# Self and causal attention of a 12-stage decoder: head rows stacked through a DRAM image, heads on the row halves

## The chip, the cores and the metric

The kernel runs on one core of a Trainium2 chip. The metric is the device time of one execution, in microseconds (us); it is a median of several runs. A core has five engines that work side by side, each through its own list of instructions in order, and wait for one another on semaphores: TensorE (PE; matmuls into PSUM, which has eight banks of 2 KB per partition), VectorE (DVE), ScalarE (ACT), GpSimd (POOL) and SyncE (SP, which here only starts DMA transfers). PEld is TensorE's loading of the stationary operand, which runs beside its matmuls.

## The reference

A decoder of four layers on x of 4 batches x 512 positions x 128 features. Each layer has three steps (an attention, a step with the context, a feed-forward part), and each step ends with `x = layernorm(x + step(x))`. Two of the twelve steps concern us, both with 16 heads of width 8: the attention of layer 1 (plain) and that of layer 3 (causal, with a softmax of its own).

```python
q, k, v = heads(x @ w_q), heads(x @ w_k), heads(x @ w_v)      # (4, 16, 512, 8)
attn = einsum('bhqd,bhkd->bhqk', q, k) * 8 ** -0.5
# layer 1: softmax(attn)
# layer 3: attn = where(causal, attn, -inf); a = clip(attn, -100, 100); m = max(a)
#          e = exp(a - m); p = e / (sum(e) + 1e-6) + 1e-8; p = p / sum(p)
out = merge_heads(einsum('bhqk,bhkd->bhqd', p, v)) @ w_proj
```

## The kernel before

The twelve steps are stages, one after the other. `attention16` is the stage of both attentions: "l1a" in the names of its tiles is the self attention (about 284 to 589 us of the profile), "l3a" the causal one (about 1486 to 1804). Constants for both are made in the first stage, the charge attention ("l0a").

**Numbers in three parts.** The scores are made by bf16 matmuls, although q and k are f32. So q and k of a batch are split into three bf16 parts, high, middle and low (tile `parts`), and a head's score is the sum of six products of parts. These lie under each other in the contraction: a head takes 64 rows, eight of width 8, six with products, one for the row maximum, one empty. Two heads, a pair, fill the 128 rows of QS (queries) and KS (keys). In KS each head of a pair has a copy of its own in which the other head's 64 rows are zero; a matmul over 128 rows then gives one head's scores.

**Units.** A batch has 4 groups of 4 heads (2 pairs); with 4 batches a stage has 16 groups, m = 0 to 15. The work is cut into units, and each engine goes through the same list of units:
- J: projections of a batch. J0 and J1 make q and k (f32 matmuls), J2 makes v, and along them ScalarE and VectorE make the three parts; J4 makes the last low part; J3 (causal) sums v.
- Q and K (L586): the rows of one pair are put in their places. Three matmuls with a constant 0/1 matrix (`k.gather`) move the parts to their rows in PSUM; ScalarE copies them to QS (L742) and KS (L753, L755), in the self attention VectorE copies the second half of KS (L843).
- A (L611): scores of 128 queries against all keys, for the two heads of a pair, into two banks; VectorE takes the row maxima (L855). The causal one has fewer keys and adds a mask (L613).
- P, T: the four heads' maxima are split into three parts (L867 to L873), turned by TensorE (L619) and added into the row of QS meant for them (L878, "the T addition").
- B (L640): scores of one head, transposed, 128 keys against all queries, with the maximum subtracted in the matmul; ScalarE takes the exponential (L773). The units alternate over banks 4 and 5, and a B waits until the exponential of the B two earlier is made. L (causal) makes a lower bound in the same way, X clips (L883).
- V (L671): the exponentials times v, four heads on four column quarters of the array. F, C, W, Y, N: transposes, output projection, norm.

**The order.** `FULL` and `CAUSAL` list the units of a group by hand: kind, how many groups ahead, which. A unit `('A', 2, 0, 1)` in group m is an A of group m + 2. `FULL_BATCH` and `CAUSAL_BATCH` put the units of a batch between them: key m % 4, position, unit. So J of the next batch stands in groups with m % 4 == 2, Q and K are made two groups ahead. Banks 0/1 and 2/3 alternate between A and T units: an A waits until VectorE has read the A or T two earlier.

SP, which issues most transfers, has nothing to do in these two stages.

Of the kernel before, what the change touches and what calls it, by code (L numbers as in the profile page):

```python
# [13 lines left out]
ALU = mybir.AluOpType  # L14
ACT = mybir.ActivationFunctionType
# [18 lines left out]
BIAS_ROWS = (0, 64, 96)  # L34
SCALE = DK ** -0.5
# [144 lines left out]
class Dispatch:  # L180
# [163 lines left out]
)  # L344
CAUSAL_BATCH = {
    1: ((17, ('C', -1)),),
    2: ((1, ('J', 1, 0)), (8, ('J', 1, 1)), (10, ('J', 1, 2)), (16, ('J', 1, 3)), (17, ('J', 1, 4)), (38, ('W', -1)),),
    3: ((6, ('Y', -1)), (17, ('N', -1)),),
# [8 lines left out]
)  # L357
FULL_BATCH = {
    1: ((30, ('C', -1)),),
    2: ((0, ('J', 1, 0)), (2, ('J', 1, 1)), (3, ('J', 1, 2)), (4, ('J', 1, 4)), (32, ('W', -1)),),  # L360
    3: ((23, ('Y', -1)), (32, ('N', -1)),),
# [3 lines left out]
def attention16(k, name, w, cross=None, mask=None, causal=False):  # L365

    nc, PS = k.nc, k.PS
    crossed = cross is not None
    KT = [(0, SC)] if crossed else [(t * P, P) for t in range(NT)]  # L380
    nk = KT[-1][0] + KT[-1][1]
    LIM = 100.0 / SCALE
    ROUND = len(KT)
    NG = BT * G
    AHEAD = 3 if crossed else 2

    def a_units(m):
        if m >= NG:
            return []
        return [("A", m, 0, hp) for hp in range(2)] if crossed else [("A", m, qt, hp) for qt in range(NT) for hp in range(2)]  # L390

    def gathers(m):
        if m >= NG:
            return []
        if crossed:
            return [("Q", m, 0)] + ([("K", m, 0)] if m % 2 == 0 else [])
        return [(c, m, i) for i in range(2) for c in "QK"]

    def projections(b):
        return [("J", b, i) for i in range(4 if causal else 3)] if b < BT else []  # L400

    def extras(m):
        b, g = m // G, m % G
        put = gathers(m + AHEAD)
        old = b - 1 if b else None
        u = [("F", m - 2)] if m >= 2 else []
        if g == 0:
            u += put + projections(b + 1)
        if g == 1:
            u = ([("J", b + 1, 4)] if b + 1 < BT else []) + u + put + ([("C", old)] if b else [])  # L410
        if g == 2:
            u += put + ([("W", old)] if b else [])
        if g == 3:
            u += ([("Y", old)] if b else []) + put + ([("N", old)] if b else [])
        return u

    def spread(base, more):
        o, put = [], 0
        for i, u in enumerate(base):
            while put < len(more) and i * (len(more) + 1) >= (put + 1) * len(base):  # L420
                o.append(more[put])
                put += 1
            o.append(u)
        return o + more[put:]

    order = projections(0) + [("J", 0, 4)]
    early = [u for m in range(AHEAD) for u in gathers(m)]
    if crossed:
        order += early + a_units(0) + [("P", 0)] + a_units(1) + [("T", 0)]
    else:  # L430
        order += early[:4]
        rest = early[4:]
        for u in a_units(0):
            order += [u] + rest[:1]
            rest = rest[1:]
        order += rest + [("P", 0), ("T", 0)]
    head = len(order)
    for m in range(NG if crossed else 0):
        base = []
        nxt = a_units(m + 2)  # L440
        base += [("P", m + 1)] if m + 1 < NG else []
        base += [("B", m, 0, 0)] + nxt[:1] + [("B", m, 0, 1)]
        base += [("T", m + 1)] if m + 1 < NG else []
        base += [("V", m - 1, 0, 1)] if m else []
        base += [("B", m, 0, 2)] + nxt[1:] + [("B", m, 0, 3)]
        order += spread(base, extras(m))
    if crossed:
        order += [("F", NG - 2), ("V", NG - 1, 0, 1), ("F", NG - 1)]
    else:
        group, batch = (CAUSAL, CAUSAL_BATCH) if causal else (FULL, FULL_BATCH)  # L450
        done = set(order)
        for m in range(-1, NG + 2):
            for i, (kind, ahead, *which) in enumerate(group):
                for at, (what, later, *part) in batch.get(m % G, ()) if 0 <= m < NG else ():
                    if at == i and 0 <= m // G + later < BT:
                        order.append((what, m // G + later, *part))
                u = (kind, m + ahead, *which)
                if 0 <= m + ahead < NG and u not in done:
                    order.append(u)
    order += [(c, BT - 1) for c in "CWYN"]  # L460
    count = lambda kinds: {u: i for i, u in enumerate([u for u in order if u[0] in kinds])}
    in_pairs = "ATQ" if crossed else "AT"
    ua, ut = count(in_pairs), count("AT")
    first_a, last_a = {}, {}
    for u in ut:
        if u[0] == "A":
            first_a.setdefault(u[1], u)
            last_a[u[1]] = u
    ub, uq, uk, uj = count("BL"), count("QK"), count("K"), count("J")
    pairs = [u for u in order if u[0] in in_pairs]  # L470
    singles = [u for u in order if u[0] in "JQKFCWN" and u not in ua and u[0:1] + u[2:] != ("J", 4)]
# [5 lines left out]
    last_b = lambda m: ub["B", m, len(KT) - 1, HG - 1]  # L477
    gathered = {b: max(i for u, i in uq.items() if u[1] // G <= b) + 1 for b in range(BT)}
    sets = 2 if crossed else 3
    freed = {}  # L480
# [5 lines left out]
    def body(block, projected, high_made, rest_made, middle_made, low_made, zeroed, v_taken, stack_ready, taken_a,  # L486
# [22 lines left out]
        def keys(m):  # L509
            return KS[:, m // G % 2 if crossed else 0]  # L510

        @block.tensor
        def _(pe):
# [3 lines left out]
            def emptied(u):  # L517
# [5 lines left out]
                if kind == "J" and u[2] == 2:  # L523
                    pe.wait_ge(v_taken, m + 1)
# [3267 lines left out]
```

## Time and profile before

| | |
|---|---|
| time, median of 3 runs | 2075.52 us (2074.79 to 2079.33) |
| profiled execution, span from first to last instruction | 2076.9 us |
| TensorE busy | 1713.3 us, 82% |
| VectorE busy | 1420.7 us, 68% |
| ScalarE busy | 1103.9 us, 53% |
| GpSimd busy | 412.8 us, 20% |
| mean granted TensorE clock | 0.912 of full speed |

The profile is of one execution. Its own time is the span; nothing else of it is shown around the span, and it lies 1.4 us over the median. Busy time is the union of an engine's instructions; matmuls are pipelined, so TensorE counts as busy while the tail of a matmul runs beside the next one. The granted clock has two levels, 0.5 (1.2 GHz) and 1.0 (2.4 GHz); values between are means. The shares are means over twelve stages with different limits, so the stages concerned have to be read by themselves.

### The profile page before, as it was taken

How to read it: one execution, taken by the hardware profiler on the slowest of the kernel's cores; microseconds unless marked ns; L12 is line 12 of the kernel's file. 1: busy time of each engine (PE TensorE's matmuls, PEld its weight loads, DVE VectorE, ACT ScalarE, POOL GpSimd, SP SyncE). 2: the span in 40 equal slices, each digit the busy share in tenths (PEclk: the TensorE clock that was granted, in tenths of full speed). 3: DMA queues.
4: the chain of work that ended last, by engine and by line, in shares of the span. 5: the costliest groups of instructions: out<-in, count | busy, mean ns of one | idle time of the engine just before them, and what ended most of it. 6: DMA issues, size and time to landing. Idle time of an engine off the chain costs nothing. (4 is left out here: it accounts for less than half of the span.)

```text
span 2076.9 us, 33295 instructions
## 1 busy us (share of the span) xinstructions
PE 1713.3 (82%) x11716; PEld 1018.4 (49%) x11806; DVE 1420.7 (68%) x3271; ACT 1103.9 (53%) x2329; POOL 412.8 (20%) x576
## 2 busy tenths in 40 slices
PE   5779869999968999994879899984489889798692
PEld 3546533333356666662734445442344445465572
DVE  4646677888765777774746767676789999666434
ACT  3436536777723444544445555652368778375362
POOL 0110030000032666653100000001300000100375
PEclk8989879999978999996979999997699999899696
DMA  4000000000025888861000000000000000000313
GB/s 123 1 1 2 1 1 1 1 1 1 1 92 217 311 327 325 331 253 42 1 0 1 1 1 1 1 1 18 0 1 2 1 1 2 1 2 7 101 52 85
DMA packets 38398, 120.09 MB, mean 58 GB/s; under 512 B 6610, under 2 KB 22139, under 8 KB 33147
## 3 DMA queue, kind: packets, MB, share of 16 engines
q1 hardware_dynamic: 28059, 104.78, 14.0%
q0 software_dynamic: 4992, 10.23, 1.6%
q10 hardware_dynamic: 5184, 2.95, 0.5%
q8 instruction: 97, 1.59, 0.3%
q14 instruction: 66, 0.54, 0.1%
HBM read 108.08 MB, written 14.58 MB: 59 GB/s over the span
## 5 line engine op out<-in xcount | busy, mean ns | idle before, releaser
L160 POOL TENSOR_SCALAR rstd<-MV 128x2 f32<-128x2 f32 (+1 forms) x100 | 25.7, 257 | 1014.9 <-DVE MV L128 1010.1
L855 DVE TENSOR_REDUCE l1aM<-PS 128x2 f32<-128x1024 f32 x128 | 152.9, 1220 | 24.1 <-PE PS L611 22.1
L773 ACT ACTIVATE l1aE<-PS 128x512 f32<-128x512 f32 x256 | 140.8, 595 | 48.3 <-PE PS L640 45.0
L773 ACT ACTIVATE l3aE<-PS 128x512 f32<-128x512 f32 (+3 forms) x256 | 102.5, 443 | 46.9 <-PE PS L644 43.9
L2737 ACT COPY PT<-PS 128x512 f32<-128x512 f32 x128 | 69.2, 589 | 93.6 <-PE PS L2648 93.3
L855 DVE TENSOR_REDUCE l3aM<-PS 128x2 f32<-128x256 f32 (+3 forms) x128 | 101.1, 818 | 18.8 <-PE PS L613 17.7
L2827 DVE TENSOR_REDUCE M<-PS 128x1 f32<-128x589 f32 x128 | 92.4, 763 | 27.1 <-PE PS L2637 26.8
L1868 PE MATMUL PS<-WB,H 128*128 128x512 f32 x234 | 109.0, 602 | 0.0
L2743 ACT ACTIVATE E<-PS,M 128x589 f32<-128x589 f32 x128 | 95.8, 762 | 17.6 <-DVE M L2827 17.5
L883 DVE SCALAR_TENSOR_TENSOR l3aE<-l3aE,l3aLB 128x2048 f32<-128x2048 f32 (+1 forms) x64 | 94.9, 1483 | 2.7 <-ACT l3aE L773 2.7
L2008 ACT ACTIVATE H<-PS,WB 128x128 f32<-128x128 f32 x156 | 44.5, 368 | 89.3 <-PE PS L1856 89.2
L611 PE MATMUL PS<-l1aKS,l1aQS 128*128 128x512 bf16 x249 | 77.4, 391 | 16.1 <-DVE l1aQS L878 5.5
L640 PE MATMUL PS<-l1aQS,l1aKS 128*128 128x512 bf16 x239 | 82.3, 387 | 5.4 <-ACT l1aE L773 4.2
L2665 PE MATMUL PS<-PT,Va 128*64 128x512 f32 x320 | 82.8, 616 | 0.8 <-ACT Q L2748 0.8
L2648 PEld LDWEIGHTS PS<-cols_const_sb,E 128*128 128x128 f32 x512 | 58.2, 144 | 49.6 <-DVE E L2847 29.4
L162 POOL TENSOR_TENSOR rstd<-rstd,mhalf 128x2 f32<-128x2 f32 (+1 forms) x100 | 75.8, 758 | 8.3
L2637 PE MATMUL PS<-K,Q 64*128 64x512 f32 x256 | 75.1, 664 | 0.0
L2021 ACT ACTIVATE A<-PS,WB 128x128 f32<-128x128 f32 x156 | 58.7, 457 | 29.3 <-PE PS L1878 29.3
L2648 PE MATMUL PS<-cols_const_sb,E 128*128 128x128 f32 x512 | 71.4, 283 | 2.8 <-DVE E L2847 2.6
L640 PE MATMUL PS<-l3aQS,l3aKS 128*128 128x512 bf16 (+3 forms) x254 | 70.3, 305 | 3.3 <-ACT l3aE L773 1.7
L2847 DVE TENSOR_SCALAR E<-E,sums 128x589 f32<-128x589 f32 x128 | 67.6, 528 | 4.5
L611 PE MATMUL PS<-l3aKS,l3aQS 128*128 128x256 bf16 (+3 forms) x248 | 62.3, 304 | 8.9 <-DVE l3aM L855 5.6
(687 smaller groups left out, 4502.8 us busy)
## 6 DMA issues: line engine op xcount, KB each, us to landing
WB<-in_experts SPq DMA_DIRECT2D x39, 1286.0 KB
TB<-mixed_tails SPq DMA_DIRECT2D x39, 768.5 KB, 7.1
ALL<-in_experts SPq DMA_DIRECT2D x8, 384.0 KB, 6.5
mixed_tails<-in_tails SPq DMA_DIRECT2D x1, 2305.5 KB, 11.9
cols_fold_sb<-in_cols_fold SPq DMA_DIRECT2D x1, 1676.0 KB, 11.5
mixed_tails<-in_tails SPq DMA_DIRECT2D x1, 1537.0 KB, 16.1
mixed_tails<-WB SPq DMA_DIRECT2D x2, 768.5 KB, 4.6
cols_l2x_sb<-in_cols_l2x SPq DMA_DIRECT2D x1, 1154.0 KB, 10.9
```

The costliest lines, as they stand in the source:

```text
L162: g.tensor_tensor(out, out, self.mhalf[:, 0:out.shape[1]], ALU.pow).then_inc(done, 1)
L611: ins = mm(o, QS[:, pp, qt * P:(qt + 1) * P], keys(m)[:, pp, par, 0:kc], start=True, stop=not causal)
L640: ins = mm(o, keys(m)[:, pp, par, k0:k0 + kn], QS[:, pp, q0:S], start=True, stop=not (mask or causal))
L773: nc.scalar.activation(E[0:kn, home(m, kt) + j, q0:S], PS[0:kn, 4 + n % 2, q0:S], ACT.Exp, scale=SCALE).then_inc(exp_done, 1)
L855: v.tensor_reduce(M[:, m % 2, qt, 2 * hp:2 * hp + 2], PS[:, bank:bank + 2, 0:kc], AX, ALU.max, negate=True).then_inc(pair_free, 1)
L883: v.scalar_tensor_tensor(e, e, 1.0, LB[:, m % 2, :, kt * P:S], ALU.min, ALU.max).then_inc(clipped, 1)
L1868: mm(o, H1[:, i % 3, c * P:(c + 1) * P], mid_w(i, c), start=False, stop=False)
L2637: ins = mm(PS[:, at_ + 2 * par, :], Q[own, b % 2, pp, q], K[own, b % 2, pp, :], start=True, stop=True)
L2648: ins = nc.tensor.transpose(PS[:, at_ + 2 * par, t * P:(t + 1) * P], E[:, ring(x, par), e0:e0 + P], k.ident)
L2665: ins = mm(PS[64 * par:64 * par + 64, 6, :], Va[:, b % 2, t, h * DH:(h + 1) * DH], PT[:, n % 2, par, t, :], start=(t == 0), stop=(t == len ...
L2743: nc.scalar.activation(E[:, i, 0:NK], scores(s, par), ACT.Exp, bias=M[:, i:i + 1], accum_out=sums[:, i:i + 1]).then_inc(exp_done, 1)
L2827: ins = v.tensor_reduce(M[:, i:i + 1], scores(s, par), AX, ALU.max, negate=True)
```

## The change

Q and K units go, with the constant matrices. The parts are written by SP to an image in DRAM, `k.image[batch, q or k, head, d, slot, position]` in bf16, each part to the slots that need it (`IMAGE_SLOTS`: the high part of q to slots 0, 3 and 6, and so on; one transfer writes a part to all its slots). Rows of 1 KB. Then SP reads a group's rows back, already stacked: one transfer of 256 KB into QS, one of 256 KB (self) or two of 128 KB (causal) into KS. The slots 5 and 7 are filled once, in the first stage: zeros for q and for k's slot 7, in k's slot 5 ones for d < 3 and zeros otherwise. An A waits on its group's transfers. The reads of group m + 4 wait until the B of group m are done.

In the self attention KS loses its zero halves: A and B of a head work on 64 of the 128 rows, the first head of a pair on rows 0 to 63, the second on 64 to 127. The causal one keeps the 128 rows.

J moves from groups with m % 4 == 2 to those with m % 4 == 1; the v projection is now J5, behind most of the group's units. The other units keep their order.

```diff
+IMAGE_SLOTS = (((0, 3, 6), (1, 4), (2,)), ((0, 1, 2), (3, 4), (6,)))
+AUG_SLOT = 5
 CAUSAL_BATCH = {
-    1: ((17, ('C', -1)),),
-    2: ((1, ('J', 1, 0)), (8, ('J', 1, 1)), (10, ('J', 1, 2)), (16, ('J', 1, 3)), (17, ('J', 1, 4)), (38, ('W', -1)),),
+    1: ((11, ('J', 1, 0)), (13, ('J', 1, 1)), (15, ('J', 1, 2)), (17, ('J', 1, 4)), (17, ('C', -1)), (20, ('J', 1, 5)), (24, ('J', 1, 3))),
+    2: ((34, ('W', -1)),),
 FULL_BATCH = {
-    1: ((30, ('C', -1)),),
-    2: ((0, ('J', 1, 0)), (2, ('J', 1, 1)), (3, ('J', 1, 2)), (4, ('J', 1, 4)), (32, ('W', -1)),),
+    1: ((0, ('J', 1, 0)), (2, ('J', 1, 1)), (3, ('J', 1, 2)), (4, ('J', 1, 4)), (24, ('J', 1, 5)), (26, ('C', -1))),
+    2: ((28, ('W', -1)),),
...
+    rows_of = lambda par: slice(0, P) if causal else slice(64 * par, 64 * par + 64)
+    order = [("J", 0, i) for i in (0, 1, 2, 4, 5)] + [("J", 0, 3)] * causal
+    order += [("A", 0, qt, hp) for qt in range(NT) for hp in range(2)] + [("P", 0), ("T", 0)]
...
+        KS = k.sb(name + "KS", [P, H // 2, 2, S] if causal else [P, H // 2, S], BF16)
+        @block.sync
+        def _(sp):
+            sp.wait_ge(k.blanked, 16 * 2 * BT)
+            for m in range(NG):
+                b, g = divmod(m, G)
+                if g == 0:
+                    for part, made in enumerate((high_made, middle_made, low_made)):
+                        for c in range(2):
+                            slots = IMAGE_SLOTS[c][part]
+                            step = slots[1] - slots[0] if len(slots) > 1 else 1
+                            rows = k.image[b, c, :, :, slots[0]:slots[-1] + 1:step, :].rearrange("h d j s -> (h d) j s")
+                            sp.wait_ge(made, 2 * b + c + 1)
+                            sp.dma_start(rows, parts[:, c, part:part + 1, :].broadcast_to([P, len(slots), S])).then_inc(imaged[c], 16)
+                    sp.wait_ge(q_imaged, PARTS * (b + 1))
+                    sp.wait_ge(k_imaged, PARTS * (b + 1))
+                if m >= G:
+                    sp.wait_ge(s_ready, last_b(m - G) + 1)
...
+                sp.dma_start(QS[:, own, :], k.image[b, 0, heads].rearrange("(a r) d j s -> (r d j) a s", r=2)).then_inc(stacked[g], 16)
+                if causal:
+                    for par in range(2):
+                        sp.dma_start(KS[64 * par:64 * par + 64, own, par, :], key[par]).then_inc(stacked[g], 16)
+                else:
+                    sp.dma_start(KS[:, own, :], k.image[b, 1, heads].rearrange("(a r) d j s -> (r d j) a s", r=2)).then_inc(stacked[g], 16)
...
                 elif kind == "A":
+                    pe.wait_ge(stacked[g], ROWS * (m // G + 1))
-                            ins = mm(o, QS[:, pp, qt * P:(qt + 1) * P], keys(m)[:, pp, par, 0:kc], start=True, stop=not causal)
+                        own = rows_of(par)
+                        key = KS[:, pp, par, :] if causal else KS[own, pp, :]
+                        ins = mm(o, QS[own, pp, qt * P:(qt + 1) * P], key[:, 0:kc], start=True, stop=not causal)
...
+        def blank_image(sp):
+            sp.wait_ge(blank_made, 1)
+            for b in range(BT):
+                for c in range(2):
+                    sp.dma_start(k.image[b, c, :, :, AUG_SLOT:DK:2, :].rearrange("h d j s -> (h d) j s"), blank[:, c]).then_inc(k.blanked, 16)
...
-            terms = one.enter_context(nc.sbuf_tensor("terms", [P, 6 * P + 2 * P + H // 2 + 1], F32))
+            terms = one.enter_context(nc.sbuf_tensor("terms", [P, 2 * P + 1], F32))
+            blank = one.enter_context(nc.sbuf_tensor("blank", [P, 2, 2, S], BF16))
```

B changes as A does. In the first stage ScalarE's eight multiplications that made the gather matrices (L3550) go, VectorE makes one small addition for the fill, GpSimd zeroes it at the start, and the load `terms` shrinks from 516.5 KB to a quarter. In l1a GpSimd no longer zeroes KS.

## Rows read from the trace of the kernel before

**Rows 1.** Busy time: us; PE, PEld, DVE, ACT, POOL (count); granted clock, DMA, GB/s

```profile
313.00:575.00 262.00, 239.95 (x1404) 96.94 (x1430) 216.78 (x307) 187.64 (x345) 5.60 (x12) 0.98 0.00 1
...
1519.00:1790.00 271.00, 245.26 (x2326) 132.08 (x2362) 249.85 (x419) 203.65 (x432) 5.86 (x12) 0.99 0.01 1
```

**Rows 2.** T addition (L878): ns min/median/max, first and last start

```profile
L878 DVE TENSOR_TENSOR l1aQS<-PS,l1aQS x16: 1212/1214/1225, 309.8 to 560.7; 128x1024 bf16<-128x1024 f32 x16
```

**Rows 3.** Busy time of l1a, from one T addition to the next

```profile
395.61:411.19 15.58, 14.50 (x86) 5.51 (x86) 13.45 (x18) 11.29 (x22) 0.00 (x0) 1.00 0.00 1
411.19:431.12 19.93, 18.02 (x104) 7.91 (x106) 16.64 (x23) 14.36 (x27) 0.00 (x0) 1.00 0.00 1
431.12:448.23 17.11, 15.96 (x100) 7.07 (x101) 16.42 (x33) 12.05 (x23) 1.86 (x4) 1.00 0.01 2
```

**Rows 4.** Timeline of TensorE, plain l1a group: start, us, engine, line, out<-in, xcount

```profile
397.85 1.92 PE L671 MATMUL PS<-l1aE,l1aVa 128*32 128x512 f32 x16
...
399.93 0.59 PE L611 MATMUL PS<-l1aKS,l1aQS 128*128 128x512 bf16 x2
400.36 0.38 PE L640 MATMUL PS<-l1aQS,l1aKS 128*128 128x512 bf16 x1
400.58 0.81 PE L586 MATMUL PS<-l1aparts,gather 128*128 128x512 bf16 x3
```

**Rows 5.** Timeline of VectorE in l1a; in brackets idle before and releaser

```profile
317.17 1.23 DVE L855 TENSOR_REDUCE l1aM<-PS 128x2 f32<-128x1024 f32 x1 [2.69 <-PE PS L611]
...
400.56 1.22 DVE L855 TENSOR_REDUCE l1aM<-PS 128x2 f32<-128x1024 f32 x1 [1.48 <-PE PS L611]
...
404.62 0.76 DVE L843 TENSOR_SCALAR l1aKS<-PS,isaug 64x512 bf16<-64x512 f32 x1
405.41 2.36 DVE L855 TENSOR_REDUCE l1aM<-PS 128x2 f32<-128x1024 f32 x2
...
420.37 0.68 DVE L812 TENSOR_TENSOR l1aparts<-l1aleft,l1aparts 128x512 bf16<-128x512 f32 x1
```

**Rows 6.** Busy time of a plain group of l3a

```profile
1653.47:1669.40 15.93, 14.75 (x147) 7.84 (x148) 14.94 (x25) 12.71 (x27) 0.00 (x0) 1.00 0.01 1
```

**Rows 7.** Timeline of VectorE in that l3a group

```profile
1657.69 0.42 DVE L855 TENSOR_REDUCE l3aM<-PS 128x2 f32<-128x256 f32 x1 [0.64 <-PE PS L613]
```

**Rows 8.** Timeline of TensorE in the latent attention

```profile
1201.06 1.13 PE L2601 MATMUL PS<-LT,cols_l2x_sb 128*128 128x512 f32 x2
...
1205.44 0.23 PE L2634 MATMUL PS<-kmask_b,ones_b 128*128 128x154 bf16 x1
1205.61 0.70 PE L2637 MATMUL PS<-K,Q 64*128 64x512 f32 x2
```

**Rows 9.** Timeline of the head of l1a

```profile
291.91 0.68 DVE L812 TENSOR_TENSOR l1aparts<-l1aleft,l1aparts 128x512 bf16<-128x512 f32 x1
...
295.78 0.59 PE L611 MATMUL PS<-l1aKS,l1aQS 128*128 128x512 bf16 x2 [0.94 <-DVE l1aKS L843]
...
313.01 1.06 PE L640 MATMUL PS<-l1aQS,l1aKS 128*128 128x512 bf16 x2
```

**Rows 10.** DMA issues: queue, count, KB each, us to landing

```profile
expert_rows<-X SPq DMA_DIRECT2D x1, 1024.0 KB, 6.4
...
terms<-in_terms ACTq DMA_DIRECT2D x1, 516.5 KB
...
cols_l3a_sb<-in_cols_l3a SPq DMA_DIRECT2D x1, 257.0 KB, 2.9
```

**Rows 11.** Timeline, end of the charge attention and start of the next stage

```profile
134.19 1.76 ACT L3550 ACTIVATE gather<-terms 128x768 bf16<-128x768 f32 x2
...
136.24 1.37 PE L989 MATMUL PS<-CT,cols_l0x_sb 128*128 128x308 f32 x2 [2.57 <-PEq L87]
```

**Rows 12.** Waits at the start: who for whom, us, times, longest

```profile
PE PS L3500 <- DMA X<-in_x: 10.5, 1, 10.5
```

**Rows 13.** Busy time of a stretch of the charge attention

```profile
60.00:80.00 20.00, 14.74 (x93) 10.76 (x92) 12.71 (x34) 8.57 (x15) 2.18 (x4) 1.00 0.01 1
```

More of the change, by code:

```diff
@@ L399, in projections @@
[L399 to L436, printed above, removed]
@@ L437, in attention16 @@
-    head = len(order)
[L438 to L459, printed above, removed]
@@ L460, in attention16 @@
-    order += [(c, BT - 1) for c in "CWYN"]
[L461 to L471, printed above, removed]
+    PARTS = 3 * 16
@@ new lines, in attention16 @@
+    ROWS = 3 * 16 if causal else 2 * 16
+    rows_of = lambda par: slice(0, P) if causal else slice(64 * par, 64 * par + 64)
+    order = [("J", 0, i) for i in (0, 1, 2, 4, 5)] + [("J", 0, 3)] * causal
+    order += [("A", 0, qt, hp) for qt in range(NT) for hp in range(2)] + [("P", 0), ("T", 0)]
+    head = len(order)
+    group, batch = (CAUSAL, CAUSAL_BATCH) if causal else (FULL, FULL_BATCH)
+    done = set(order)
+    for m in range(-1, NG + 2):
+        for i, (kind, ahead, *which) in enumerate(group):
+            for at, (what, later, *part) in batch.get(m % G, ()) if 0 <= m < NG else ():
+                if at == i and 0 <= m // G + later < BT:
+                    order.append((what, m // G + later, *part))
+            u = (kind, m + ahead, *which)
+            if 0 <= m + ahead < NG and u not in done:
+                order.append(u)
@@ L472, in attention16 @@
+    order += [(c, BT - 1) for c in "CWYN"]
+    count = lambda units: {u: i for i, u in enumerate(units)}
+    ut, ub = (count([u for u in order if u[0] in kinds]) for kinds in ("AT", "BL"))
+    uj = count([u for u in order if u[0] == "J" and u[2] not in (2, 4)])
+    pairs = list(ut)
+    last_a = {u[1]: u for u in ut if u[0] == "A"}
+    singles = [u for u in order if u in uj or u[0] in "FCWN"]
     ring = (7, 4, 5, 6)
@@ L526, in emptied @@
                     pe.wait_ge(v_summed, m + 1)
-                if kind in "QK":
-                    pe.wait_ge(taken_a, uq[u] + 1)
-                if kind == "K" and not causal:
-                    pe.wait_ge(taken_v, uk[u] + 1)
                 if kind in "AT":
@@ L572, in _ @@
                         ins.then_inc(projected, 1)
-                elif kind in "QK":
-                    b, isk = m // G, int(kind == "K")
-                    for part, made in enumerate((high_made, middle_made, low_made)):
-                        pe.wait_ge(made, 2 * b + isk + 1)
-                    if not crossed:
-                        outs = [(2 * g + u[2], PS[:, own, 0:width[isk]])]
-                    elif isk:
-                        outs = [(2 * g + i, PS[:, own, i * nk:(i + 1) * nk]) for i in range(HG)]
-                    else:
-                        outs = [(2 * g + i, PS[:, bank + i, :]) for i in range(2)]
-                    for pp, o in outs:
-                        for part in range(3):
-                            ins = mm(o, k.gather[:, pp, isk, part, :], parts[:, isk, part, 0:width[isk]],
-                                     start=(part == 0), stop=(part == 2))
-                    ins.then_inc(stack_ready, 1)
@@ L589, in _ @@
                 elif kind == "A":
                     _, _, qt, hp = u
-                    if ut[u] == 0:
-                        pe.wait_ge(zeroed, 2)
-                    if u == first_a[m]:
-                        mine = [x for x in gathers(m) + (gathers(m - 1) if crossed and m % 2 else [])]
-                        pe.wait_ge(taken_a, max(uq[x] for x in mine) + 1)
-                        if not causal:
-                            pe.wait_ge(taken_v, max(uk[x] for x in mine if x in uk) + 1)
@@ new lines, in _ @@
+                    pe.wait_ge(stacked[g], ROWS * (m // G + 1))
+                    pp = 2 * g + hp
+                    kc = (qt + 1) * P if causal else S
+                    for par in range(2):
+                        o = PS[:, bank + par, 0:kc]
+                        own = rows_of(par)
+                        key = KS[:, pp, par, :] if causal else KS[own, pp, :]
+                        ins = mm(o, QS[own, pp, qt * P:(qt + 1) * P], key[:, 0:kc], start=True, stop=not causal)
+                        if causal:
+                            ins = mm(o[:, qt * P:kc], k.ident_b, k.causal_b, start=False, stop=True)
@@ L757, in _ @@
+                        nc.scalar.copy(parts[:, i - 1, 1, :], left[:, i - 1, :]).then_inc(middle_made, 1)
                 elif kind in "BL":
@@ L865, in _ @@
                     maxima, rest = (a.rearrange("p t (a r) -> p a t r", a=2) for a in (Mg, Mleft[:, :, :]))
-                    high, middle, low = (Mp[:, :, :, 32 + i:P:64] for i in range(3))
+                    high, middle, low = (Mp[:, :, :, DK * i + AUG_SLOT:P:64] for i in range(3))
                     step(v.tensor_copy(high, maxima))
```

266 lines of the change are left out of this document (83 added, 183 removed), and 14 rows, old and new, of tables (CAUSAL, FULL).

## The prediction

> **What bounds the kernel now.** The changed function runs twice: the self attention (stage l1a) and the causal attention (l3a). First I read the sums by stretch [rows 1]: over its steady part l1a has TensorE busy 240 of 262 us and VectorE 217; l3a has VectorE busy 250 of 271 and TensorE 245. A busy TensorE overstates itself, because matmuls overlap. So next comes the period. Each of the 16 groups has one T addition on VectorE, the first at 309.8 and the last at 560.7 us [rows 2], 250.9 us for 15 intervals. Cut at these additions there are three kinds [rows 3]: a plain group takes 15.6 us (nine of them, 15.1 to 15.6), one with the next batch's projections 19.9 (three, and the first group of the stage takes 19.8), the one after that 17.1 (two); the last takes 13.1.
>
> For a plain group of l1a the starts on TensorE give what each unit holds the engine for [rows 4]: an A pair 0.43 us (399.93 to 400.36), a B 0.22 (400.36 to 400.58), a gather three times that, 0.65, a V of 16 matmuls 1.9. With 8 A, 16 B, 4 gathers and 2 V that is 3.4 + 3.5 + 2.6 + 3.8 = 13.3 us, before the short transposes of T and F: TensorE is nearly full. VectorE in the same group is busy 13.45 us [rows 3] and waits in two places for A's matmuls; the long wait, 1.48 us at 400.56, is the time that the V ahead of that A takes [rows 5]. So a plain l1a group is held by TensorE, with VectorE two microseconds behind. In l3a a plain group of 15.93 us has VectorE busy 14.94 [rows 6], with one visible wait of 0.64 [rows 7]: there VectorE is the bound.
>
> **What the change takes away.** Per group and stage: 12 gather matmuls (2.6 us of TensorE), two ScalarE copies to QS, and in l1a two ScalarE and two VectorE copies to KS; in l3a four ScalarE copies. VectorE's copies take 0.76 us each; the one at 404.62 holds VectorE to 405.41, so 0.79, 1.55 to 1.6 per group [rows 5]. In l3a VectorE loses nothing.
>
> In l1a a pair of A, and neighbouring B of a pair, use the array's two row halves. Does that run side by side? The latent attention already has it, in f32: two 64-row matmuls of 512 columns take 0.70 us together, two full-array ones of as many columns 1.13 [rows 8]. So the second starts about 0.1 us after the first and not after its whole pass. For the bf16 A pair I take 0.1 to 0.2 us off 0.43.
>
> Here a rule speaks against the change. In the rows the switch from a 128-row to a 64-row matmul costs nothing visible: the 128-row one starts at 1205.44 and lasts 0.23, the 64-row pair starts at 1205.61 [rows 8]. The Trainium skill (TensorEngine Tiling (Array Packing), Tiling Modes, Key Properties) says that a change of tiling mode drains the engine. By it T and F, neighbours in the order, would be one more stretch in another mode, two more changes per l1a group; the time that this would give stands with the rivals.
>
> **The sum for l1a.** A plain group: minus 1.55 (K copies). The 1.48 wait stays for the most part, since the V in front of that A is unchanged and only the A pair and the B pair before it and the A pair itself get shorter: three times 0.1 to 0.2, I take 0.5. Together minus 2.1, nine times: minus 19. Bounds: minus 1.0 (a third of the copies' time comes back as new waits) and minus 3.3 (the copies, and nearly all 2.1 us of idle [rows 3]). The three groups with projections: VectorE is busy 16.64 of 19.93 and its gaps are the to and fro with ScalarE over the three-part split, which stays; minus 1.8 each, 5.4. The two after them: VectorE busy 16.42 of 17.11, so only the copies go: minus 1.6 each, 3.2. The first group waits longer (2.69 us at 317.17 [rows 5]): minus 2.5. The last: minus 0.3. Sum minus 30.
>
> **The head of a stage** gets longer. Before, the last low part is made at 292.6 (291.91 + 0.68) and the first A starts at 295.78 [rows 9]. After, six image writes of 1536 KB in all go out behind the parts, then two reads of 256 KB. Nearest rows: a write of 1024 KB lands in 6.4 us, a read of 257 KB in 2.9 [rows 10]. 768 KB (the high parts) leave before the middle parts are made, so I let the writes end 4 us after the last low part (between 2.5 and 8, the latter at 1024 KB per 6.4 us with no head start), and the reads 4 us later (the second queues behind the first): first A at 300.6, 5 us late. From there the head is shorter: the first B came 17.2 us after the first A [rows 9], with four gathers and two K copies (1.6 us of VectorE) among the A units, which go. Net plus 3 (0 to plus 8). In l3a, where VectorE had nothing to lose but waited for the gathers, plus 0.5 (minus 1 to plus 4), kept inside that stage's term.
>
> At the later batches the round trip is hidden. The projections move one group forward. Before, the last low part came about 10 us after the T that opens the interval (420.37 plus 0.68 against 411.19 [rows 3, 5]; the VectorE copy of V ahead of it is moved behind): then 8 us for write and read give 18 us. The first A of the next batch is due just before the end of the interval after, 18 + 13 - 3 = 28 us after that T. Cover: some 10 us; if the round trip grows by more, VectorE stands still there. The reads of the other groups are issued when the B of the group four earlier are done, more than one period before they are needed. SP has nothing else in these stages; behind its waits stand only its own image transfers. Three transfers a group on l3a, two on l1a, cost the computing engines nothing but a wait on a semaphore.
>
> **l3a.** VectorE is full, so only its waits can go: 0.64 in a plain group [rows 7]. ScalarE loses its copies (off the path), TensorE 2.6 us; the A units come earlier. I take a half, with the longer waits of the three batch groups: minus 4 (plus 4 to minus 10).
>
> **Edges.** Eight ScalarE multiplications that made the gather matrices go. The last two stand between the charge attention's last copy and its end: 1.76 us from 134.19, and the next stage's first matmul at 136.24 had waited for that [rows 11]: minus 1.7. The others lie beside TensorE work. Added there are one small VectorE addition (hidden, the engine then waits for ScalarE), a GpSimd fill at the start, idle otherwise, and eight fills of the image, 2 MB, with the DMA engines idle and hundreds of microseconds of cover. At the start the first matmul waits 10.5 us for x [rows 12] while a load of 516.5 KB shares the DMA engines; 388 KB of it go, 2.4 us at the rate of the 1024 KB write [rows 10] and nothing if the two don't meet: I take minus 0.7, nearer to nothing, because it is one of many loads.
>
> **Together**: -30 + 3 - 4 - 2.4 = -33 us on the profiled execution, whose span is 2076.9 us with nothing to add around it that the profile shows; it lies 1.4 us over the median of the runs, 2075.5. Forecast: 2042 us.
>
> **Rivals.**
> (1) *VectorE closes up.* TensorE, some 10 us of work in a 13 us group, runs ahead, and the wait behind V goes too: 3.3 in nine groups, 3 in the three with projections, l3a minus 8: about 2020. For it: TensorE gets 4 us of slack. Against: units stand in a written order, and A behind V can't be moved forward. 0.22.
> (2) *Waits come back.* B alternates over two banks and each waits for the exponential two earlier; A stands behind B in the order, so the freed VectorE time turns into waits for A: minus 1 a group, nothing in l3a, heads 3 us longer each: 10 + 4 + 6 more, 2062. 0.16.
> (3) *Slower: the round trip is late.* The place is the first A of each batch. It decides from 18 us for write and read (8 estimated, 10 of cover). At 26 us six batches stand still for 8 us, and the two heads 18 us longer: 48 + 36 more, 2126; at 18 the heads alone take 20 of the 33, and from about 20 us the kernel is slower than before. For it: 128 KB and 256 KB transfers in rows of 1 KB, a write and a read that must follow each other. Against: the 1024 KB write of 6.4 us has rows of 512 bytes. 0.05.
> (4) *Slower: the clock falls.* At 1.2 GHz TensorE would need twice its 9.8 us and the transposes twice, 21 us where 15.6 sufficed: over l1a plus 88 in place of minus 30, 2160. It decides from somewhat over a quarter of the stage. Against: with TensorE busy 14.7 of 20 us, 74%, the granted clock was 1.00 [rows 13], about the share that I expect (10 of 13.4). 0.04.
> (5) *The halves don't overlap, or the mode change costs.* Without overlap (the change then does not do what it says) the 0.5 per group and as much in the others is lost: 2048. A drain, priced by the tail of a matmul (0.38 long, the next after 0.22 [rows 4]: 0.16), is 0.3 us a group with two more changes, 5 us in 16: 2047 if TensorE is on the path there. Both together 0.10. This second part is what the named rule of the Trainium skill would give.
>
> The forecast itself has 0.43. Its own range is 2031 to 2051; over all, 2018 to 2064 leaves out (3), (4) and the outer parts of (1) and (2). A difference of under 0.2%, 4 us, is what a measurement can't tell from none. Faster by more: (1), (5), the forecast and nearly all of (2): 0.88. Slower: (3), (4) and a little of (2): 0.09. Same: 0.03.
>
> **What would show it.** Right: T additions of l1a 13.3 to 13.7 us apart in plain groups, with one VectorE wait of about a microsecond behind V; the two matmuls of an A starting about 0.1 us apart; l3a plain groups still 15.4 to 15.9; the first A of l1a some 8 us after the last low part (3.2 before), and no later wait of A for a DMA; granted clock 1.00 between. Wrong: plain groups over 14.5, TensorE waiting for the stacked rows at the batch changes, or a granted clock well under 0.9.

## The result and the profile after

The changed kernel takes 2061.5 us (median of four runs, 2060.1 to 2070.3) where the kernel before takes 2077.4 beside it: ratio 0.9928, 95% interval 0.9909 to 0.9947. It is faster by 0.7%, about 16 us; forecast were 33, to 2042. The profiled execution of the changed kernel has a span of 2068.3 us; it is the longest of the four, so the stages below are compared by their own landmarks and not by the span.

The landmarks are the T additions again, now L733. In both kernels there are sixteen in each stage, and fifteen intervals between them: in the self attention (l1a) these sum to 224.6 us after 250.9, in the causal attention (l3a) to 273.2 after 262.6. So one stage gained 26.3 us and the other lost 10.6: together 15.7, about the difference of the medians. Each sum is of one execution.

These are the busy times of the changed kernel between T additions (us; PE, PEld, DVE, ACT, POOL with counts; granted clock, DMA share, GB/s): in l1a a plain group, the group with the projections and the one behind it, which answer to [rows 3]; then in l3a a plain group, which answers to [rows 6], a group with the projections, and a second plain group.

```profile
372.58:385.25 12.67, 10.99 (x78) 3.65 (x76) 11.61 (x17) 9.25 (x18) 0.00 (x0) 1.00 0.13 41
385.25:404.01 18.76, 13.89 (x78) 4.02 (x76) 14.35 (x21) 11.26 (x21) 0.00 (x0) 0.91 0.35 114
404.01:419.14 15.13, 13.15 (x92) 5.09 (x92) 12.39 (x17) 10.06 (x19) 0.00 (x0) 1.00 0.12 36
1563.94:1580.07 16.13, 13.47 (x139) 7.35 (x137) 14.94 (x24) 9.49 (x23) 0.00 (x0) 0.96 0.11 34
1580.07:1606.93 26.86, 19.54 (x160) 11.18 (x160) 19.80 (x33) 11.74 (x26) 0.00 (x0) 0.87 0.24 79
...
1641.48:1656.97 15.49, 12.70 (x136) 6.86 (x136) 14.74 (x25) 9.04 (x22) 0.00 (x0) 1.00 0.13 35
```

A plain l1a group fell from 15.58 to 12.67 us; of the five plain groups left in the stage four take 12.7 to 12.8, the fifth, at a granted clock of 0.88, 14.32. The first plain l3a group shown did not fall: VectorE is busy 14.94 us in it, exactly as in [rows 6], and the clock is 0.96. The second took 15.49 us, 0.44 less than before, at a clock of 1.00. Most of them had a clock of 0.90 to 0.96 and took 15.9 to 16.5 us. The causal projection group takes 26.86 us; before, the three of that stage took 21.7 to 21.9. Its excess over a plain group nearly doubled, and the granted clock in it is 0.87 (over the stage's intervals 0.92, before 0.98).

TensorE and VectorE in the plain l1a group (timeline: start, us, engine, line, out<-in, xcount, in brackets idle before and releaser), which answer to [rows 4] and [rows 5]:

```profile
374.39 1.92 PE L578 MATMUL PS<-l1aE,l1aVa 128*32 128x512 f32 x16
376.25 0.39 PE L551 MATMUL PS<-l1aQS,l1aKS 64*128 64x512 bf16 x1
...
380.58 0.39 PE L521 MATMUL PS<-l1aKS,l1aQS 64*128 64x512 bf16 x2
380.81 0.38 PE L551 MATMUL PS<-l1aQS,l1aKS 64*128 64x512 bf16 x1
```

```profile
376.90 2.50 DVE L710 TENSOR_REDUCE l1aM<-PS 128x2 f32<-128x1024 f32 x2 [0.83 <-PE PS L521]
```

The two matmuls of an A pair, one on each row half, take 0.39 us together, as long as one alone; on the full array a pair took 0.59 [rows 4]. VectorE's wait behind V fell from 1.48 to 0.83 us.

At the heads the first A waits for the stacked rows. This is who TensorE waits for (us in total, times, longest), the two rows with the image:

```profile
PE PS L521 <- DMA l1aKS<-head_image: 9.1, 1, 9.1
PE PS L521 <- DMA l3aKS<-head_image: 4.1, 1, 4.1
```

It happens once in each stage; at the later batches TensorE never waits for the image. The wait for x at the start fell from 10.5 [rows 12] to 9.7, and at the end of the charge attention the multiplications of [rows 11] are gone: ScalarE's last copy starts at 135.80, takes 0.58, and the next stage's first matmul follows at 136.69, 0.31 us after the copy's end (before 1.96).

### The profile page after: what moved, and what is told of

Same layout as the page of the kernel before. It is cut to its first block and busy times, and to the rows that moved or that the text cites. A ratio compares the mean times of both kernels' runs of the same rounds, so it can differ in the third digit from the quotient of the medians.

```text
span 2068.3 us, 32399 instructions
## 1 busy us (share of the span) xinstructions
PE 1655.5 (80%) x11422; PEld 981.1 (47%) x11422; DVE 1393.1 (67%) x3239; ACT 1006.6 (49%) x2161; POOL 407.1 (20%) x573
## 5 line engine op out<-in xcount | busy, mean ns | idle before, releaser
L710 DVE TENSOR_REDUCE l3aM<-PS 128x2 f32<-128x256 f32 (+3 forms) x128 | 100.1, 817 | 14.6 <-PE PS L523 14.6
L2597 ACT ACTIVATE E<-PS,M 128x589 f32<-128x589 f32 x128 | 95.8, 762 | 17.6 <-DVE M L2681 17.5
L551 PE MATMUL PS<-l1aQS,l1aKS 64*128 64x512 bf16 x256 | 83.9, 405 | 20.2 <-ACT l1aE L649 17.4
L551 PE MATMUL PS<-l3aQS,l3aKS 128*128 128x512 bf16 (+3 forms) x256 | 76.0, 319 | 10.8 <-ACT l3aE L649 10.1
L521 PE MATMUL PS<-l1aKS,l1aQS 64*128 64x512 bf16 x256 | 61.5, 426 | 23.3 <-DVE l1aM L710 9.5
L521 PE MATMUL PS<-l3aKS,l3aQS 128*128 128x128 bf16 (+3 forms) x256 | 66.5, 315 | 14.8 <-DVE l3aM L710 9.5
```

Source lines behind the costliest of these rows:

```text
L521: ins = mm(o, QS[own, pp, qt * P:(qt + 1) * P], key[:, 0:kc], start=True, stop=not causal)
L551: ins = mm(o, key[:, kt * P:(kt + 1) * P], QS[own, pp, q0:S], start=True, stop=not causal)
L710: v.tensor_reduce(M[:, m % 2, qt, 2 * hp:2 * hp + 2], PS[:, bank:bank + 2, 0:kc], AX, ALU.max, negate=True).then_inc(pair_free, 1)
L2597: nc.scalar.activation(E[:, i, 0:NK], scores(s, par), ACT.Exp, bias=M[:, i:i + 1], accum_out=sums[:, i:i + 1]).then_inc(exp_done, 1)
```

## Where the causal stage lost it

TensorE and VectorE in the causal projection group of the changed kernel, the waits and what stands around them:

```profile
1587.70 1.13 PE L500 MATMUL PS<-XT,cols_l3a_sb 128*128 128x512 f32 x2 [1.97 <-DVE R L759]
...
1590.48 1.10 PE L500 MATMUL PS<-XT,cols_l3a_sb 128*128 128x512 f32 x2 [0.95 <-DVE l3aleft L683]
...
1600.50 2.05 PE L508 MATMUL PS<-l3aVa,cols_const_sb 128*128 128x128 f32 x8 [2.93 <-DVE l3aVa L694]
...
1603.77 1.93 PE L578 MATMUL PS<-l3aE,l3aVa 128*32 128x512 f32 x8
```

```profile
1596.47 2.28 DVE L738 SCALAR_TENSOR_TENSOR l3aE<-l3aE,l3aLB 128x2048 f32<-128x2048 f32 x1
...
1599.67 0.68 DVE L694 COPY l3aVa<-PS 128x512 f32<-128x512 f32 x1
...
1606.93 1.22 DVE L733 TENSOR_TENSOR l3aQS<-PS,l3aQS 128x1024 bf16<-128x1024 f32 x1 [2.39 <-PE PS L529]
```

Two places of the hand-written list show. First, q's projection (place 11) stands right behind F (place 10). Both use PSUM bank 7, so TensorE stands 1.97 us until VectorE has read F's result (its last reading instruction writes R, L759), and k's projection then 0.95 us for q. Second, the sum of v (L508, place 24) needs VectorE's copy of v (L694). That copy has its place behind the clip X (2.28 us) and the split of the maxima, so TensorE stands 2.93 us; every B behind it waits too, and at the end VectorE itself waits 2.39 us for the T matmuls.

The granted clock falls inside that second wait, which begins at 1597.57 and ends at 1600.50 (busy times as above):

```profile
1596.00:1598.00 2.00, 1.56 (x18) 0.73 (x16) 2.00 (x2) 1.37 (x4) 0.00 (x0) 1.00 0.38 124
1598.00:1601.00 3.00, 0.50 (x2) 0.53 (x3) 2.83 (x8) 0.38 (x1) 0.00 (x0) 0.74 0.28 78
1601.00:1604.00 3.00, 2.85 (x18) 2.02 (x20) 2.19 (x4) 0.82 (x3) 0.00 (x0) 0.50 0.30 99
```

So the wait has a second price: the eight matmuls of V behind it take 1.93 us, where in a projection group of the kernel before, at a clock of 1.00, they took 1.06.

A projection group and the one behind it take 40.5, 43.3 and 41.3 us at the three batch changes, where before a plain group and the projection group behind it took 37.0, 37.7 and 37.7: 12.8 us more. The other nine intervals of the stage gave 2.1 back.

The theory: these places are the loss. Rivals: (a) TensorE, thinner by the gathers, is granted a lower clock there, and that alone is the loss; (b) the image's transfers in that group delay something.

## The experiments

All are edits of the changed kernel. The table has, for each, the sum of the fifteen intervals of each stage in its profiled execution, the median and the ratio to the kernel before on the same chip.

| kernel | l1a sum | l3a sum | median, us | ratio (95% interval) |
|---|---|---|---|---|
| before | 250.9 | 262.6 | 2077.4 | 1 |
| changed | 224.6 | 273.2 | 2061.5 | 0.9928 (0.9909 to 0.9947) |
| a: projections ahead of F | 224.6 | 264.1 | 2056.3 | 0.9887 (0.9852 to 0.9921) |
| b: only q, k ahead of F | 224.3 | 269.4 | 2057.7 | 0.9892 (0.9864 to 0.9920) |
| c: only v a group later | 224.7 | 264.7 | 2050.1 | 0.9877 (0.9841 to 0.9912) |
| d: causal A twice | 224.7 | 278.3 | 2067.0 | 0.9948 (0.9930 to 0.9966) |
| f: b and c together | 224.5 | 261.7 | 2053.3 (1 run) | |
| g: zero halves, l1a | 223.0 | 273.0 | 2056.9 | 0.9929 (0.9901 to 0.9957) |
| h: image written twice | 220.9 | 270.9 | 2067.2 (1 run) | |
| i: late subtraction, v later | 214.4 | 267.5 | 2050.5 | 0.9896 (0.9869 to 0.9923) |
| l: l1a A twice | 218.5 | 272.9 | 2054.3 | 0.9889 (0.9860 to 0.9918) |
| j: i's l1a, f's l3a | 214.7 | 261.9 | 2041.5 | 0.9834 (0.9808 to 0.9860) |
| k: j, l1a A twice | 218.7 | 264.3 | 2043.3 | 0.9834 (0.9805 to 0.9863) |

Medians of one kernel's runs scatter by 5 us and more, so most intervals overlap; the sums of a stage whose code is untouched repeat within a microsecond in all kernels but h (3.7 and 2.3 off) and k (2.4 off in l3a), and they carry the verdicts. A difference of 2 to 4 us between two sums, such as b's, is therefore near to what one execution can be off. In the diffs a unit is written short, J0 for `('J', 1, 0)`.

**a, all projections ahead of F.**

```
-    1: ((11, J0), (13, J1), (15, J2), (17, J4), (17, C), (20, J5), (24, J3)),
+    1: ((1, J0), (3, J1), (5, J2), (6, J4), (6, J5), (9, J3), (17, C)),
```

> Causal attention only: in the group of the projections all six steps of the next batch's projections are put ahead of F (places 1 to 9 of the group's list in place of 11 to 24), among them v and its sum. Theory (the place costs: q and k wait for F's reading of PSUM bank 7, the sum of v waits 2.93 us for VectorE's copy of v behind the clip and the maxima's split): the three projection groups of the causal stage, 24.21, 26.86 and 25.77 us in the changed kernel, fall to about 21.8 each, as before; the stage's sum of intervals 273.2 -> about 262, the kernel 2061.5 -> about 2050. Rival one (TensorE, thinner without the gathers, is granted .87 of its clock there, and this alone makes the groups long): the groups stay at 24 to 27 and the clock at about .87; about 2061. Rival two (the transfers of the image in that group delay something): they are as many and start earlier, 2060 to 2062.

The three groups took 21.42, 23.67 and 23.66 us, the stage 264.1: 9.1 of the 10.6 us are back, with the place alone. The clock in the middle one rose from 0.87 to 1.00 without any work added. Together with the fall inside the wait, shown above, that says that there it followed the waits:

```profile
1574.87:1598.54 23.67, 17.31 (x160) 9.82 (x160) 19.64 (x34) 12.45 (x28) 0.00 (x0) 1.00 0.27 90
```

**b and c, the two places apart.** b has J0, J1, J2, J4 as in a, and J5, J3 at 20 and 24; c has the first four as in the changed kernel and J5, J3 in the next group:

```
+    2: ((1, J5), (6, J3), (34, W)),
```

> Causal attention only: of the projections' steps, q and k with their splits are put ahead of F (places 1 to 6), v and its sum stay at places 20 and 24. Theory: TensorE's waits at q and k (1.97 and 0.95 us in one group) go, the wait of 2.93 us for the copy of v stays; each projection group shorter by 2 to 3 us, 2061.5 -> about 2054. If the place of v is the whole cause: 2060 to 2062. If the clock is the cause: 2060 to 2062.

> Causal attention only: q and k stay where the change put them (places 11 to 17 of the group), v and its sum move to the next group, places 1 and 6, ahead of that group's F. Theory: the wait of 2.93 us for the copy of v goes with the slow 1.93 us of the products of V behind it, the projection group falls by about 4.5 us, the next one, which now has v's copy and two additions, grows by about 2.5; three times -2, 2061.5 -> about 2055. If q and k's waits behind F are the whole cause: the sum of the two groups stays, 2060 to 2062. If the clock is the cause: 2060 to 2063.

b gives 3.8 us of the stage and c 8.5. In c the projection group falls from 26.86 to 21.65 and the next grows from 16.39 to 18.06. TensorE's waits in the causal stage, first of the changed kernel, then of c, show which went:

```profile
PE PS L508 <- DVE l3aVa L694: 9.9, 3, 4.1
...
PE PS L500 <- DVE R L759: 3.9, 2, 2.0
...
PE PS L500 <- DVE l3aleft L683: 2.8, 3, 0.9
```

```profile
PE PS L500 <- DVE R L759: 3.9, 2, 2.0
...
PE PS L500 <- DVE l3aleft L683: 2.8, 3, 0.9
```

The 9.9 us for the copy of v are gone in c, the others stand as they were. So the place of v is the larger part, about two thirds, and the wait behind F the smaller. Both include what the clock gives back: in c's three projection groups it is 0.94 to 1.00, in the changed kernel 0.86 to 0.93.

**f, both.** J0, J1, J2, J4 at places 1, 3, 5, 6; J5, J3 in the next group at 1 and 6.

> Causal attention only: q and k ahead of F in the projection group (places 1 to 6) and v with its sum in the next group, ahead of its F (places 1 and 6). If the waits for F and for v are separate terms, the projection group falls to about 20 to 21 and the next one holds 18; the sum of the stage's intervals 262 or a little less (273.2 in the changed kernel, 264.1 and 264.7 with one remedy each); the kernel about 2050. If one remedy already took what the other would take: 264 to 265, about 2052.

261.7: the two remedies, 3.8 and 8.5, give 11.5 together, nearly their sum. They are separate terms. The stage is then as long as before (262.6) and no shorter.

**d, the clock by itself in the causal stage.**

```
-        ins = mm(o, QS[own, pp, ...], key[:, 0:kc], start=True, stop=not causal)
+        for again in range(2 if causal and g in (1, 2) else 1):
...
+            ins = mm(o, QS[own, pp, ...], key[:, 0:kc], start=True, stop=not causal or not last)
```

> Causal attention only: in the groups that issue their A products for heads groups 1 and 2 each product of a pair is computed twice into the same bank (the first result is written over), which keeps TensorE busy where the gathers did before. Rival one (the granted clock is the cause): the clock in the projection groups rises from .87 towards .97, and they fall by 2 us or more each; 2061.5 -> about 2055. Theory (place): the clock may rise, but the waits for F and for v stay, the groups stay within 1 us or grow with the products' own time; 2061 to 2068.

The middle group took 28.08 us, at a clock of still 0.87; the stage's mean rose from 0.92 to 0.94 and its sum by 5.1 us. In the first projection group the clock did rise, from 0.86 to 0.93, and the group stayed as long (24.13 us after 24.21). As a test of the clock this is inconclusive: in the middle group it didn't move, and the added products take time themselves.

**g, self attention with zero halves.** KS has two images again, each product runs over 128 rows; stacking and order stay.

```
-    rows_of = lambda par: slice(0, P) if causal else slice(64 * par, 64 * par + 64)
+    rows_of = lambda par: slice(0, P)
...
```

> Self attention only: the keys keep two images with a zero half each and every product runs over all 128 rows, as in the causal attention; the stacking through DRAM and the order stay. Theory (two products on the row halves run side by side, 0.39 us for both): eight pairs a group cost 0.43 to 0.59 us more each on TensorE, which is busy 10.99 of 12.67 us, so a plain group grows to about 14 to 14.5, the stage by about 20 us, and the kernel goes from 2061.5 to about 2080. Rival (VectorE sets the plain group at 12.7 and TensorE has room): plain groups 12.7 to 13, the kernel 2061 to 2066.

Both theories failed. A plain group took 13.53 us, 0.86 more, but the projection groups took 17.1 to 17.6 in place of 18.8 to 19.7, and the sum is 223.0 against 224.6. The row halves give nothing in the sum here, although the pair is faster on them. The projection group of g and the plain one before it:

```profile
368.85:382.38 13.53, 12.57 (x76) 4.37 (x77) 11.74 (x17) 9.38 (x18) 0.00 (x0) 1.00 0.13 39
382.38:399.94 17.56, 14.38 (x78) 4.76 (x77) 14.34 (x20) 11.55 (x21) 0.00 (x0) 1.00 0.37 121
```

VectorE has the same work (14.34 us against 14.35); the clock is 1.00 where the row halves had 0.91. In the changed kernel one V of that group takes 3.14 us, in g each takes 1.92.

**l, the clock by itself in the self attention.**

```
-                    for par in range(2):
+                    for par in (0, 1) if causal or g != 2 else (0, 1, 0, 1):
```

> Self attention only, order and row halves as in the changed kernel: the A products of the heads group that is prepared in the projection group are each computed twice (the first results are written over), some 3 us more of TensorE where it is busy 13.9 of 18.8 us. With zero halves everywhere the clock in that group was 1.00 and the group took 17.56 us, with row halves .91 and 18.76 us. Theory (in the self attention the row halves leave TensorE so thin that its clock falls in the projection group, and that gives their gain back): the clock there rises to 1.00, the slow products of V (3.14 us for 16) take 1.92, the three groups fall by 1 us or more each, plain groups stay 12.66; 2061.5 -> about 2057. Rival (the zero halves' gain there had another reason, or the added products cost what the clock gives): groups at 18.5 to 20, 2061 to 2066.

The groups took 17.07, 17.56 and 17.56 us where the changed kernel has 19.15, 18.76 and 19.65, with more work for TensorE:

```profile
381.52:399.08 17.56, 13.69 (x93) 4.15 (x89) 14.22 (x21) 11.52 (x21) 0.00 (x0) 1.00 0.37 121
```

The sum fell by 6.1 us (the last three intervals came out 2.0 longer). So in the self attention the clock is a cause, where in the causal stage it went with the waits. That is where the gain of the row halves went: against g, which has full rows and a clock of 0.98 over the stage (l 0.96), l is 4.5 us shorter.

**h, the round trip made longer.**

```
+    sp.dma_start(k.image2[b, c, ...], parts[:, c, part:part + 1, :]...).then_inc(imaged[c], 16)
...
```

> Both attentions: every write of the image is issued a second time, to another DRAM tensor, ahead of its own write, so the six writes take twice as long and the stacked rows land about 6 us later. Theory (behind the two heads the round trip is covered by a whole group): the intervals between additions stay within 0.3 us, and only the heads grow, by 3 to 6 us each; 2067 to 2073. Rival (the round trip is late for the next batch's first A): the group behind each projection group grows by 3 to 6 us too, six times; 2085 to 2105.

The heads grew: the two waits for the image are 13.1 and 8.1 us, 4.0 more each, and from a stage's first matmul to its first T addition it takes 29.6 and 28.7 us, where the changed kernel has 25.4 and 25.0. No other wait for the image appears, and no group behind a projection group grew by more than 0.2 us. The doubled writes are covered at all later batches, and rival (b) falls. The expected 0.3 us was too narrow all the same: single intervals differ by minus 1.7 to plus 1.2 us, and the self attention even came out at 220.9. What differs can be seen in one plain group, with the same instructions in both kernels, first of the changed one, then of h:

```profile
434.00:448.32 14.32, 12.97 (x82) 4.11 (x79) 11.61 (x17) 9.03 (x17) 0.00 (x0) 0.88 0.13 37
```

```profile
433.75:446.41 12.66, 11.33 (x82) 3.92 (x79) 11.60 (x16) 9.03 (x17) 0.00 (x0) 1.00 0.13 42
```

A clock of 0.88 in place of 1.00 cost this group 1.66 us. A plain group of the causal stage shows the same, again first of the changed kernel:

```profile
1716.44:1732.98 16.54, 13.81 (x136) 7.36 (x136) 14.83 (x25) 8.85 (x20) 0.00 (x0) 0.90 0.10 33
```

```profile
1716.95:1732.43 15.48, 12.64 (x135) 6.87 (x136) 14.74 (x25) 9.03 (x22) 0.00 (x0) 1.00 0.13 35
```

It costs 1.06 us there, so the clock has its part in the causal stage too, outside the projection groups. Why it fell in one execution and not in the other is open.

**i, j, k: a better order.** i makes VectorE's subtraction (the rest of q and k) a step of its own, J6 and J7, some places behind the product:

```
+ FULL_BATCH    1: ((0, J0), (2, J6), (5, J1), (8, J7), (8, J2), (12, J4), (26, C)),  2: ((5, J5), (28, W)),
+ CAUSAL_BATCH  1: ((1, J0), (5, J6), (5, J1), (9, J7), (9, J2), (12, J4), (17, C)),  2: ((1, J5), (6, J3), (34, W)),
```

> Both attentions: in the projection group VectorE's subtraction for q's and k's rest is a step of its own, put behind the maxima of one or two A products, k's product is issued later, and v comes in the next group, ahead of its F. It is taken from the idle times of VectorE in the projection groups (2.00 and 0.95 us behind ScalarE's rounding, in the self attention and in the causal one). Theory (what the projection groups cost over a plain group is these idle times and the place behind F, not the clock): the self attention's groups fall from 18.8 to about 16.5 and the causal ones to about 19.5, three each, and the groups behind them grow by 1 to 2 in the causal stage; the kernel about 2045. Rival (the clock, or the transfers): the sums stay, 2050 to 2062.

The self attention fell to 214.4 (projection groups 16.70, 17.57, 17.13, the ones behind them 13.6 to 13.8 in place of 15.1). Which of i's two moves there, the late subtraction or v, gives how much was not tried apart. The causal stage has 267.5, worse than f, and its projection groups take 21.4 to 23.4 us where 19.5 was expected: there the late subtraction holds bank 7 to the place just before F (in the middle one F starts at 1578.25, 0.1 us after the subtraction for k ends, and TensorE has stood 1.22 us). Hence j, with i's self attention and f's causal order:

> The self attention's order of the kernel with the late subtraction (sum of the stage's intervals 214.4) and the causal order with q and k ahead of F and v in the next group, with the subtraction at once (261.7). If the two stages do not touch each other: 214 and 262, the kernel about 6 us under the one with the late subtraction in both, 2044 to 2047. If the causal stage's 267.5 against 261.7 was chance and not the place: about 2050.

214.7 and 261.9, and 2041.5 us: the fastest, about 20 us under the changed kernel by the medians. Its middle projection group of l1a still has a clock of 0.90:

```profile
379.64:397.22 17.58, 14.34 (x80) 4.21 (x78) 14.36 (x21) 11.34 (x22) 0.00 (x0) 0.90 0.37 121
```

> The kernel with both orders, and in its self attention the A products of the projection group computed twice. If the clock is what is left there: the three projection groups of the self attention, about 17.5 at a clock of .90, fall to 16 to 16.5, the kernel by 3 us under the one without; otherwise equal or up to 3 us more.

The middle group fell to 16.66 at a clock of 1.00, but one plain group rose from 12.7 to 14.2 and the last three intervals by 3.5 together, the sum from 214.7 to 218.7; the ratio is the same. Doubled work is no remedy in this order.

## Why the prediction was wrong

**The step that failed is the l3a term**, "I take a half, with the longer waits of the three batch groups: minus 4 (plus 4 to minus 10)". It came out at plus 10.6, beyond its bounds, and the 14.6 us between are most of the 17 that the forecast was off. Its half about plain groups (0.64 of wait [rows 7]) came true only at full clock: 15.49 us for 15.93, but up to 16.54 at a clock of 0.90. The larger miss is that "the projections move one group forward" was worked out for the transfers behind them alone. What they are moved next to in the causal list was not priced: F with its PSUM bank ahead of q, and X with the split ahead of v's copy. The runs show both terms, 3.8 and 8.5 us (b, c), 11.5 together (f); the clock that falls inside the wait is part of their price.

**The self attention's term was near in sum, by errors that cancel.** Without the head, minus 30 was forecast and minus 26.3 measured. The sum counts nine plain groups; there are eight among the fifteen intervals, so its own figures give minus 28. Four of them fell by 2.8 to 2.9 and not 2.1, within the far bound of 3.3; a fifth fell by 1.3, at a clock of 0.88. The first group of the stage fell by 5.6 and not 2.5. Against that, the three projection groups, "minus 1.8 each", fell by 0.3 to 1.2, and the group behind each of them, which has v's products now, takes 15.1 us, half a microsecond less than a plain one before and not 2.1. l shows that the clock took at least what the projection groups lack, since with doubled products two of them took 17.56 us, 2.4 under [rows 3]. Rival (4), the clock, was priced as a fall over the whole stage; it fell in single groups, at 1.1 to 2.1 us each (18.76 and 19.65 against 17.56, 14.32 against 12.66, 16.54 against 15.48). Over the intervals the mean was 0.92 in both stages, where the prediction named 1.00 as a sign of being right.

**Row halves.** They do run side by side (0.39 for a pair). The new changes between full rows and row halves cost nothing visible. Behind T the first 64-row B starts 0.54 us after T's start:

```profile
384.00 0.61 PE L529 MATMUL PS<-ident_b,l1aMp 128*128 128x128 bf16 x8
384.54 0.60 PE L551 MATMUL PS<-l1aQS,l1aKS 64*128 64x512 bf16 x2
```

In the kernel before, with B on all rows, it was 0.69 (410.00 to 410.69). The V on all rows that starts at 374.39 lasts 1.92 us as before [rows 4], and the 64-row products behind it start at 376.25, 1.86 after its start (before 1.85). The Trainium skill (TensorEngine Tiling (Array Packing), Tiling Modes, Key Properties) says that changing the tiling mode drains TensorE; no time for that shows in these rows. But the row halves are worth nothing in the sum (g), which I had not thought of: the part of rival (5) in which they don't help is true for another reason than that rival's.

**Heads, hidden round trip, edges.** The self attention's head was forecast at plus 3: from the stage's first matmul to the first T addition it took 25.4 us after 25.0, plus 0.4. The first A came 2.3 us later in the stage (13.3 after its start, before 11.0), not 5: it starts 6.1 us behind the last low part (293.1 to 299.2), where 8 were estimated. The first read is issued 2.5 us after that part is made, where the writes had been given 4, and the first A follows 3.5 later, where the reads had been given 4. In l3a the head is equal, 25.0. That the round trip is hidden later is shown by h. The waits at the edges fell by 0.8 (x) and 1.65 (the charge attention's multiplications), as forecast. That the whole got shorter by as much is not shown: the self attention's first matmul comes at 285.9 us after 284.8 before, and between 281.8 and 285.9 in the twelve kernels that have the change, so this stretch varies by more than that between executions.

With the causal list in a better order, and the self attention's too, the kernel takes 2041.5 us, near the forecast. That is chance: the self attention gains 36 us where 30 was forecast, the causal stage 1 and not 4.

## What to carry to other kernels

When a step of a hand-written order moves, price its new neighbours, not only what it feeds: which bank it shares with the unit ahead of it, and what stands ahead of its readers in each engine's own queue. Taking work off an engine that does not set a stage's period gives little there (0.4 us in a plain causal group at full clock); read the period's engine in each stage by itself before giving both the same gain. And a thinner TensorE may be granted a lower clock in the groups in which it waits, which can return what was saved (with row halves 0.82 to 0.91 in the projection groups of l1a, with full rows 1.00); look at the granted clock group by group.

## What the runs showed of the hardware

- Two bf16 matmuls of 64 rows and 512 columns, one on each row half and into two banks, take 0.39 us together; on all rows one after the other 0.59.
- The same instructions can be granted different clocks in two executions: a self attention group took 14.32 us at 0.88 and 12.66 at 1.00, a causal one 16.54 at 0.90 and 15.48 at 1.00.
- In the causal projection group the granted clock was 1.00 until 1598 us and 0.50 from 1601 to 1604; the engine had stood still from 1597.57 to 1600.50.
- A write of 384 KB of the DRAM image landed in 2.5 to 2.6 us and a read of 256 KB into 128 partitions in 2.8 to 3.1 (medians; 4.5 and 5.7 at the head of l1a, where eight reads follow each other). The write has about the rate of the 1024 KB in 6.4 us in [rows 10], on which the head was estimated.
